# Cross-attention layers 2 and 3 and the MLP without barriers, with weights split ahead in a buffer of their own

## What is computed

```python
h = _layer_norm(x, ln1_scale, ln1_offset)
x = res + _cross_attention(h, xf_1, wq1, bq1, wk1, bk1, wv1, bv1, wo1, bo1, bias_k1, bias_v1)
...
h = _layer_norm(x, ln_mlp_scale, ln_mlp_offset)
h = jax.nn.gelu(h @ w_fc1 + b_fc1, approximate=False) @ w_fc2 + b_fc2
return x + h
```

```python
qh = (q_in @ wq + bq).reshape(b, q_len, H, K)
kh = (kv_in @ wk + bk).reshape(b, t, H, K)
vh = (kv_in @ wv + bv).reshape(b, t, H, K)
kh = jnp.concatenate([kh, jnp.broadcast_to(bias_k, (b, 1, H, K))], axis=1)
vh = jnp.concatenate([vh, jnp.broadcast_to(bias_v, (b, 1, H, K))], axis=1)
weights = jax.nn.softmax(jnp.einsum('bqhk,bthk->bhqt', qh, kh) / scale, axis=-1)
ctx = jnp.einsum('bhqt,bthk->bqhk', weights, vh).reshape(b, q_len, H * K)
return ctx @ wo + bo
```

## Time and profile before

| | before |
|---|---|
| three runs | 1885.82 to 1887.55 us, median 1886.25 |
| profiled execution | time 1886.75 us, span 1885.0 us |
| mean TensorE clock granted | 0.968 of full speed |
| layer 1 | to 484 us |
| layer 2: norm, queries, attention, outputs | from 484, 501, 555 and 1104 us |
| layer 3: the same | from 1161, 1178, 1234 and 1783 us |
| MLP with its norm | from 1840 us to the end |

### The profile page before, as it was taken

The page is one execution under the profiler, slowest core; times in us unless marked ns, Lnnn a source line. Parts: engine busy times, 40 slices in busy tenths (PEclk is TensorE's granted clock), DMA queues, the critical chain, the costliest instruction groups (busy, mean ns, idle before and its releaser), DMA issues.

```text
span 1885.0 us, 32804 instructions
## 1 busy us (share of the span) xinstructions
PE 1713.8 (91%) x9942; PEld 1464.1 (78%) x9942; DVE 1242.0 (66%) x2455; ACT 1019.3 (54%) x1857; POOL 348.1 (18%) x285
## 2 busy tenths in 40 slices
PE   3698888897699999999999977999999999999896
PEld 3677777786478888888888865778888888888785
DVE  5577777776675666666666666856657656666574
ACT  2466666665354555555555545545555555545462
POOL 4446655531330000000000013500000000000032
PEclk8899999998899999999999998999999999999998
DMA  7776666763240110110110112421011001010021
GB/s 234 189 164 171 171 175 163 171 154 82 68 133 25 65 64 1 65 65 14 51 65 33 34 37 68 101 91 66 4 62 65 32 33 65 33 33 0 4 67 55
DMA packets 114095, 149.50 MB, mean 79 GB/s; under 512 B 25640, under 2 KB 99880, under 8 KB 114024
## 3 DMA queue, kind: packets, MB, share of 16 engines
q1 hardware_dynamic: 112680, 142.42, 27.7%
q10 hardware_dynamic: 1344, 6.19, 1.0%
HBM read 108.28 MB, written 3.42 MB: 59 GB/s over the span
## 4 chain that ended last, share of the span: by engine, by line
PE 70%; DVE 5%; issue 3%; ACT 2%; POOL 2%; SPq 1%; DMA 1%; PEld 0%; DVEq 0%; ACTq 0%; PEldq 0%; POOLq 0%
PE ps L862 16%; PE ps L635 11%; PE ps L637 11%; PE ps L636 11%; PE ps L864 8%; PE ps L835 8%; PE ps L846 1%; DVE neg L1411 1%; ACT prob L1049 1%; PE ps L717 1%; SPq L328 1%; DVE pt L1341 1%; POOL cx L607 1%; PE ps L734 1%; DMA ar<-in_wk 1%
## 5 line engine op out<-in xcount | busy, mean ns | idle before, releaser
L862 PE MATMUL ps<-cx,rr 128*128 128x512 f32 x1344 | 483.4, 402 | 3.7 <-issue 2.3
L1205 ACT ACTIVATE rr<-ps 128x512 fp32r<-128x512 f32 x336 | 201.0, 599 | 362.6 <-PE ps L835 361.1
L864 PE MATMUL ps<-cx,rr 128*128 128x256 f32 x1344 | 372.5, 277 | 0.0
L607 POOL TENSOR_TENSOR cx<-ar,cx 128x512 fp32r<-128x512 f32 x72 | 95.2, 1326 | 1235.0 <-ACT cx L1277 1234.9
L862 PEld LDWEIGHTS ps<-cx,rr 128*128 128x128 f32 x1344 | 252.2, 188 | 61.9 <-issue 8.9
L635 PE MATMUL ps<-ct,rr 128*128 128x500 f32 x672 | 280.8, 418 | 6.2 <-ACT ar L1189 6.2
L1534 DVE TENSOR_TENSOR rr<-ps,rr 128x512 fp32r<-128x512 f32 x336 | 231.7, 691 | 58.9 <-ACT rr L1205 42.0
L637 PE MATMUL ps<-ct,rr 128*128 128x500 f32 x672 | 262.0, 390 | 0.0
L636 PE MATMUL ps<-ct,rr 128*128 128x500 f32 x672 | 261.1, 389 | 0.0
L864 PEld LDWEIGHTS ps<-cx,rr 128*128 128x128 f32 x1344 | 253.2, 188 | 0.0
L1511 DVE TENSOR_REDUCE mx<-ps 128x1 f32<-128x500 f32 x336 | 227.3, 677 | 16.3 <-PE ps L637 9.4
(11 more groups left out here) (183 smaller groups left out, 3029.7 us busy)
## 6 DMA issues: line engine op xcount, KB each, us to landing
raw_t<-in_ctx_t SPq DMA_DIRECT2D x24, 1500.0 KB, 6.3
k<-khl SPq DMA_DIRECT2D x192, 187.5 KB
raw<-in_ctx SPq DMA_DIRECT2D x24, 1408.0 KB
raw<-stat_scratch ACTq DMA_DIRECT2D x7, 750.0 KB, 3.9
ar<-in_wq SPq DMA_DIRECT2D x32, 128.0 KB, 3.6
ar<-in_wk SPq DMA_DIRECT2D x32, 128.0 KB, 4.0
ar<-in_wv SPq DMA_DIRECT2D x32, 128.0 KB, 2.2
ar<-in_wo SPq DMA_DIRECT2D x32, 128.0 KB, 2.1
```

What stands on the lines that cost most here:

```text
L607: pool.tensor_tensor(w_s[:, 2 * slot + 1, :], w_raw[:, slot, :], f(w_s[:, 2 * slot, :]), ALU.subtract).then_inc(s["w_lo"], 1)
L862: pe.matmul(ps[:, 6, :], pt[0:n, 0, c, :], cx[0:n, c, :], start=c == 0, stop=False, skip_group_check=True)
L864: mm = pe.matmul(ps[:, 6, 0:D], pt[0:n, 1, c, :], cx[0:n, c, 0:D], start=False, stop=c == CH - 1, skip_group_check=True)
L1205: act.activation(pt[:, 0, GRP * k:GRP * (k + 1), :], ps[:, 3 + k, :].rearrange("p (c q) -> p c q", q=P), ACT.Copy)\
```

## The change

The barriers after layer 1 and all later ones go. `w_raw`, `w_s`, `dk_raw` and the rows `cb` get memory of their own, over buffers of layer 1 that are free by its last batch. The loops over steps are written out, and all stages share one numbering of the steps. Around this:

- In layer 1's last batch SP loads the first four steps' weights; ACT and POOL split the next context's transposed rows and three steps' weights. The same is done at each end of a stage for the stage behind it.
- The norm goes by halves: the mean product waits for each half of `xt`, DVE centres each half, ACT squares it, the sums of squares land in two banks, and the first projection waits for each half alone.
- The key product is one DVE operation per half with an accumulated sum (128 columns each), and runs up to three steps ahead. Context rows are split inside the query steps, two thirds on DVE at steps 3 and 5.
- The bias product, the first tile's scores and the turned bias row go before the last three second products; the first softmax is in step 14.
- Head 0's first output product and the transposed sums go before the last tile's weighted sum; two heads are split in the last batch. `dv_m` is made by POOL instead of DVE.

```diff
+        w_raw = sb("w_raw", [P, NS, 512])
+        w_s = sb("w_s", [P, 2 * NS, 512], F32R)
+        dk_raw = sb("dk_raw", [P, NS, 2 * P])
+        cb = sb("cb", [H, 4 * P])
...
-        w_raw = at(ar, 4032, NS, 512)
-        dk_raw = spare
...
-        w_s = at(cx_flat, 0, 2 * NS, 512)
...
+            sp.wait_ge(s["zpv"], SLOTS * (B - 1))
+            for n in range(NS):
+                step_weights("a", 1, n)
+            head_rows(1)
             for i in (1, 2):
...
+            def ct_low_next(j):
+                v = slice(SB * j, SB * (j + 1))
+                pool.wait_ge(s["ct_hi"], j + 1)
+                low(ct[:, 1, :, v], raw_t[:, :, v], ct[:, 0, :, v]).then_inc(s["ct_lo"], 1)
+            def weight_low(kind, i, n):
+                slot = n % NS
+                pool.wait_ge(s["w_hi"], BASE[kind, i] + n + 1)
+                low(w_s[:, 2 * slot + 1, :], w_raw[:, slot, :], w_s[:, 2 * slot, :]).then_inc(s["w_lo"], 1)
+            def key_bias(i, n):
+                slot = n % NS
+                pool.wait_ge(s[f"dk_in{slot}"], 32 * ((H * (i - 1) + n) // NS + 1))
+                pool.tensor_tensor(dk_raw[:, slot, 0:P], dk_raw[:, slot, 0:P], dk_raw[:, slot, P:2 * P],
+                                   ALU.subtract).then_inc(s["dk_ready"], 1)
...
                     low(wo_s[:, 1, :, :], wo_raw, wo_s[:, 0, :, :]).then_inc(s["wo_lo"], 1)
+                if kind == "plain" and t in (2, 3, 5):
+                    ct_low_next((2, 3, 5).index(t))
+                if kind == "plain" and t >= 5:
+                    weight_low("a", 1, t - 5)
+                    key_bias(1, t - 5)
...
-                step_splits("a", i, H, A_BASE[i])
-                drain(pool, 3 * i)
-                drain(pool, 3 * i + 1)
-                step_splits("o", i, H, O_BASE[i])
-                drain(pool, 3 * i + 2)
-            step_splits("m", 0, F // P, M_BASE)
-            drain(pool, 9)
+                    weight_low("o", i, n)
...
             def norm(n):
                 for e in range(DH):
+                    pe.wait_ge(s["x_ready"], DH * n + e + 1)
                     mm = pe.matmul(ps[:, 0, 0:NQ], mean_w[:, :], xt[:, e, :], start=e == 0, stop=e == DH - 1)
                 mm.then_inc(s["ln_pe"], 1)
-                pe.wait_ge(s["ln_dve"], LN_V * n + 2)
-                for c in range(NQ // QC):
-                    for e in range(DH):
-                        mm = pe.matmul(ps[0:QC, 1, c:c + 1], sq[:, e, QC * c:QC * (c + 1)], mean_w[:, 0:1],
-                                       start=e == 0, stop=e == DH - 1)
-                mm.then_inc(s["ln_pe"], 1)
-                pe.wait_ge(s["ln_dve"], LN_V * n + 4)
+                for e in range(DH):
+                    pe.wait_ge(s["ln_sq"], DH * n + e + 1)
+                    for c in range(NQ // QC):
+                        mm = pe.matmul(ps[0:QC, 1 + 2 * e, c:c + 1], sq[:, e, QC * c:QC * (c + 1)], mean_w[:, 0:1],
+                                       start=True, stop=True)
+                    mm.then_inc(s["ln_pe"], 1)
+                pe.wait_ge(s["ln_dve"], LN_V * n + 5)
                 pe.matmul(ps[:, 2, 0:NQ], mean_w[0:QC, :], diag.rearrange("p c q -> p (c q)"), start=True, stop=True)\
                     .then_inc(s["ln_pe"], 1)
-                pe.wait_ge(s["h_lo"], DH * (n + 1))
...
+            def queries(i):
+                r = i - 1
+                first_product("a", i, 0)
+                for n in range(H):
+                    if n + 1 < H:
+                        first_product("a", i, n + 1)
+                    if n == H - 3:
+                        pe.wait_ge(s["u_ready"], H * i)
+                        pe.wait_ge(s["ht_ready"], DH * i)
+                        for e in range(DH):
+                            mm = pe.matmul(ps[0:H, 7, 0:NQ], u_k[:, e, :], ht[:, e, :], start=e == 0, stop=e == DH - 1)
+                        mm.then_inc(s["small_pe"], 1)
+                    if n == H - 2:
+                        for j in range(3):
+                            if j < 2:
+                                pe.wait_ge(s["h1_lo"], BASE["a", i] + H - 1 + j)
+                            scores(r, 0, 0, 0, j)
+                        pe.wait_ge(s["small_dma"], 96 * r + 32)
...
+                                scores(r, nb, nt, g + 1, k)
+                            transposes(r, t, g, k)
+                        if end:
+                            pe.wait_ge(s["pb_ready"], i)
+                            pe.transpose(ps[0:GT, 2, 0:P], pbq[:, :], ident[:, :]).then_inc(s["small_pe"], 1)
+                        turn_output(r, g - 1)
+                        if end:
+                            first_product("o", i, 0)
+                        weighted(r, b, t, g)
+                with pe.Fori(0, B - 1) as b:
+                    batch(b, False)
+                batch(B - 1, True)
...
+            def outputs(i):
+                extra_product(i, 0)
+                first_product("o", i, 1)
+                turn_output(i - 1, GT - 1)
+                extra_product(i, 1)
+                for n in range(H):
+                    if n and n + 1 < H:
+                        first_product("o", i, n + 1)
+                        extra_product(i, n + 1)
+                    second_product("o", i, n)
...
+                    act.activation(sq[:, e, :], xc[:, e, :], ACT.Square).then_inc(s["ln_sq"], 1)
...
-                dve.tensor_tensor(dk_prod, w_raw[:, slot, 0:D].rearrange("p (e k) -> p e k", e=DH),
-                                  dk_raw[:, slot:slot + 1, 0:P].to_broadcast([P, DH, P]), ALU.mult).then_inc(s["prod_ready"], 1)
-                dve.wait_ge(s["prod_ready"], j + 1)
-                dve.tensor_reduce(u_k[:, :, bass.ds(n, 1)], dk_prod, AX.X, ALU.add).then_inc(s["u_ready"], 1)
...
+            def extra_key(i, n):
+                slot = n % NS
+                dve.wait_ge(s["dk_ready"], H * (i - 1) + n + 1)
+                if i > 1 or n:
+                    dve.wait_ge(s["u_ready"], H * (i - 1) + n)
+                for e in range(DH):
+                    ins = dve.scalar_tensor_tensor(out=dk_prod[:, e, :], in0=w_raw[:, slot, e * P:(e + 1) * P], scalar=1.0,
+                                                   in1=dk_raw[:, slot, 0:P], op0=ALU.mult, op1=ALU.mult,
+                                                   accum_out=u_k[:, e, n:n + 1])
...
+            def queries(i):
+                r = i - 1
+                extra_key(i, 0)
+                first_split("a", i, 0)
+                for n in range(H):
+                    if n + 1 < H:
+                        first_split("a", i, n + 1)
+                    for m in {0: (1,), 1: (2, 3), 2: (4, 5)}.get(n, (n + 3,) if n + 3 < H else ()):
+                        extra_key(i, m)
+                    if n == 3:
+                        split_cx(r, 0, 0)
+                    if n == 5:
+                        split_cx(r, 0, 1)
+                    if n == 7:
+                        head_constants(i)
+                    if n == H - 4:
+                        split_q(r, 0, 0)
+                        split_q(r, 1, 1)
```

741 lines of the change are left out of this document (358 added, 383 removed).

## The result

| | before | after |
|---|---|---|
| median | 1886.9 us (1885.82 to 1887.96, 4 runs) | 1865.45 us (1864.25 to 1868.23, 4 runs) |
| ratio | | 0.9886, 95% interval 0.9874 to 0.9898 |
| span of the profiled execution | 1885.0 us | 1864.4 us |
| mean TensorE clock granted | 0.968 | 0.974 |

The change makes the kernel 1.1% faster. The forecast was twice that, 1843.5 us in a range of 1832 to 1859, and the measured time lies above the range.

A forecast was written before the change was run, and what follows sets the result against it. TensorE, busy 91%, was taken as the bound, its idle time in norms, first softmax and output starts. Terms +3.9, -19.6, -5.7, -3.4, -18.0 sum to -42.8, giving 1843.5 us beside the median; range 1832 to 1859.

The forecast's parts named there:

- Layer 1, +3.9: End of layer 1: reciprocals queue behind POOL's third weight half, delaying PE 4.1 less 0.2 us; bounds 0 and 5.
- The norms, -19.6: Three layer norms, from DVE's first write of xt to PE's first projection: 11.4 us each, saving 6.8, 6.0 and 6.8.
- The diagonal: DVE operation in each norm, 3.3 to 5.0 us before: put at 1.05, 0.6 alone, bounds 0.6 and 5.0.
- The output stages, -18.0: Two stages, ACT's read of the last weighted product to xt: 47.6 us in place of 56.6, 9.0 saved twice.
- a value row: Output steps: moved from DVE to POOL, 0.5 us beside its 1.26 in a step of 2.64, taken as free.
- The attention and its start: Second tile's scores: wait of 3.03 us falls to 0.6, low-clock stretch of 5.13 to 3.4; -3.4, bounds 0 and -3.4.
- The query stages, -5.7: Layers 2 and 3, first projection to second tile's scores: 52.0 us each, against 53.6 and 56.1 before.
- 2.0 us of stall: Each query stage: PE stall from DVE's 4.8 us of new work against 4 us freed; bounds 0 and 8.7.
- the other terms: Each query stage: steps 42.8, bias product, first scores and a transpose 6.15, softmax wait 0.6, later transposes 0.45 us.
- rival 3: Weight stream not ahead: key-step buffers free late, 4 us in each of four stages, 1859.5 us; chance 0.06.
- Rival 1: DVE bounds the query steps as both fused products wait for POOL: 8.0 us a stage, 1857.5 us; chance 0.15.
- Rival 4: Slower: each fused product waits for a whole weight half, 1.26 us, steps of 4.25 us, 1897 us; chance 0.03.

The follow-up runs named there:

- e7: Changed kernel with reciprocals first in layer 1's last slot, early key products, late context split, whole rows in step 10, head constants spread: 0.9752 of before, 1839.9 us.
- e14: Changed kernel with reciprocals first, early key products, late context split, constants spread, head 1's first output product earlier, whole rows by ACT in step 3: 1836.8 us.
- e15: e7 less its late rows, so POOL makes the norm's whole rows in step 5 again: 0.9771 of the kernel before.
- e2: Changed kernel with DVE's key products of steps 0 to 3 together before its first low half, then one per step: 0.9846 of the kernel before.
- e10: e7 without the early key products of steps 0 to 3: 0.9814 of the kernel before.
- e5: Changed kernel with POOL making the norm's whole rows in step 10 in place of step 5: 0.9834 of the kernel before.
- e13: Changed kernel with the norm's whole rows made by ACT in its step 3, never by POOL: 0.983 of the kernel before.
- the repeat: The changed kernel timed again without any edit: 0.9893 of the kernel before.

## Why the prediction was wrong

**Layer 1, +3.9.** Right. The wait is 3.94 us, and undoing it gives back 4.6.

**The norms, -19.6.** Right to 1.5 us: 11.96, 11.98 and 11.73 us for 11.4. The diagonal at 0.87 us was inside its 0.6 to 1.05.

**The output stages, -18.0.** Right: 46.79 and 47.04 us behind the last read, forecast 46.8. One size in it was wrong and stayed hidden: a value row takes POOL 1.43 us (median), not 0.5, so POOL works 2.7 us in a step of 2.64 and is close to being the bound there.

**The attention and its start.** Mostly right. The first softmax is covered, the wait is 0.33 us and the clock behind it full. The stages with 1.5 us of head 0's work in them got 0.4 and 0.7 us shorter, where 0.9 was forecast.

**The query stages, -5.7.** Wrong, and with them the time: +13.0 us in the profiled executions (63.26 + 59.45 against 53.57 + 56.12). The step that failed is "Slack behind a stall is lost, so I put 2.0 us of stall on PE, bounds 0 and 8.7": against the other terms' 50.0 the stages took 13.3 and 9.5 us more, both over the bound. The other terms were fair in sum, since kernels e7, e14 and e15 reach 48.9 to 51.9. What I had costed was DVE's sum of work, and the upper bound of 8.7 has no working in the prediction. What the runs show instead is three things:

1. The weight stream wasn't ahead (rival 3, at 0.06 and 4 us a stage). A slot of step 5 waits for the key product of step 1, which I had seen, but not that the change puts it behind two low halves of DVE at the start of the stage: the issue comes at 507.88, 7 us after that of step 4 (2.9 us before the change). Freeing it gives 6.7 us in the two query stages as the only edit (e2), and 6.2 with all else mended (e10).
2. POOL's whole rows, 2.96 us, had no term in the sum, and no cover by name. Before, they stood behind step 3's low half; the change puts them behind step 5's, where POOL had just waited 3.40 us for a transfer. The prediction struck out the 0.88 us "for a missing low half" of the earlier trace rows, "since three are made ahead"; in their place came 1.47 and 1.61. That reading was wrong. The kernel before made three ahead as well, and the low half that PE waited for up to 513.68 came late because it stood behind these same rows. POOL's timeline of the kernel before:

```profile
491.56 1.26 POOL L607 TENSOR_TENSOR cx<-ar,cx 128x512 fp32r<-128x512 f32 x1
...
493.20 1.27 POOL L607 TENSOR_TENSOR cx<-ar,cx 128x512 fp32r<-128x512 f32 x1
...
494.83 1.28 POOL L607 TENSOR_TENSOR cx<-ar,cx 128x512 fp32r<-128x512 f32 x1
...
509.35 3.03 POOL L600 TENSOR_SCALAR ar<-ar,vec 128x448 f32<-128x448 f32 x2
512.35 1.27 POOL L607 TENSOR_TENSOR cx<-ar,cx 128x512 fp32r<-128x512 f32 x1
```

   So the price of the rows stood in the trace, and the change didn't remove it. Beside a late stream the rows cost 10.5 us in the two stages (e5); with the other four edits in, 1.3 (e15). By e13 it is the 3 us of a held POOL that count.
3. DVE's burst pieces met POOL's backlog. The first context third had 1.19 us in the sum and took 2.29 (the second took 1.22); the key product 0.37 and took 0.64 on average; the head constants 1.6 and took 3.1. The 1.19 of the earlier trace rows is of pieces beside an idle POOL: they ran at 548.40 to 561.72, where the earlier trace rows show POOL at 0.00.

On top of these lies the clock: in layer 2 of the changed kernel's profiled execution each wait of 2.5 us was followed by 4 to 5 us at a mean clock of 0.50 to 0.58, which the prediction had read in the earlier trace rows and then costed only behind the softmax. It isn't so behind every wait (1.00 behind 2.46 us in layer 3, and behind 2.49 us in layer 2 of the repeat), so this part of a stage's time changes from one execution to the next. No run holds the clock still, and its share of each edit's gain isn't told apart.

Parts of rivals 1 and 3 came together, of rival 3 only in the query stages: the output stages were on forecast. Rival 1 alone ends inside the range (1857.5), rival 3 half a microsecond above it (1859.5), and their sum is far outside: 14 and 16 us above the forecast give 1873.5, and 1865.45 was measured. I had given them chances as if only one could happen. Rival 4's mechanism (each key product held for a whole weight half) is real for some of them, 1.34 to 1.41 us, but not for all.

Operations of DVE with two SBUF inputs stretch beside POOL (0.29 to 1.4, 1.22 to 2.29 us), and the ones that read PSUM don't (L1699 stays at 0.67). The rule on the ports in the Trainium skill (SBUF — State Buffer, "Who interferes with whom") fits that. It would allow each of them to lose at most the length of one POOL operation, and the changed kernel's rows stay within that: 1.1 us lost beside weight halves of 1.3. The 3.3 to 5.0 us of the earlier trace rows and their fall to 0.87 say that it can be several when POOL works without a pause.

Left open: why the clock falls at one wait and not at another of the same length, and by how much each edit would gain at a steady clock.

## What to carry to other kernels

A step loop fed through a ring of buffers is a cycle across queues: find the operation that frees the buffer and the engine it stands on, and give each of them slack in its own steps: the same 3 us on POOL cost 10.5 us beside other lateness and 1.3 us without it. When an auxiliary piece of 3 us moves, ask of its engine how far ahead it is at the new place, and check it against the step length, not against the engine's mean share. Cost a PE wait like these of 2.5 us as a range, from its own length to nearly twice that, since five of seven had half clock at them or behind them. And where two rivals can happen together, give their sum a chance.

## What the hardware showed that I had not expected

- A fused multiply with an accumulated sum on DVE is followed by a separate read of the accumulator, 78 ns each; two fused operations of 128 columns cost as much as one product of 256 and a reduction (1.43 and 1.39 us).
- The value row of 80x128 takes DVE 0.27 us (median) and POOL 1.43.
- The same code has different clocks: behind TensorE waits of 2.46 and 2.50 us, 9 us apart in one stage, the granted clock was 1.00 and 0.60, and layer 1 took 480.8 and 486.0 us with the same idle time of TensorE within 0.5 us.
- The same DVE operation of 128x1024 took 1.22 us beside a POOL with pauses and 2.29 us beside one working off a backlog.
